# Regrouping the batches of a fused adaLN block (2, 4, 2 for 2, 2, 4), expert chunks of 2, 4, 1, 1 tiles, and the second modulations on ScalarE and GpSimd

## The reference

```python
mod = (_silu(L0_c) @ L0_wmod).reshape(L0_c.shape[0], 6, 1, -1)
sa, ca, ga, sb, cb, gb = (mod[:, 0], mod[:, 1], mod[:, 2], mod[:, 3], mod[:, 4], mod[:, 5])
ga = (2 * (ga >= 0) - 1) * jnp.maximum(jnp.abs(ga), 0.25)
gb = (2 * (gb >= 0) - 1) * jnp.maximum(jnp.abs(gb), 0.25)
h = _layernorm(x, axis=-1) * (1 + ca) + sa
x = x + ga * attn_ref(h, ...)
h = _layernorm(x, axis=-1) * (1 + cb) + sb
x = x + gb * ffn_ref(h, w_gate, w_up, w_down)

...
scores = (relu(x @ modr_w1 + modr_b1) @ modr_w2 + modr_b2)[..., 0]
topk_scores, topk_idx = jax.lax.top_k(scores, k)       
w = jax.nn.softmax(topk_scores, -1)
tok = take rows sorted(topk_idx); n1 = _ln(tok)
uv = n1 @ m_in_w; u, res = uv[:, :256], uv[:, 256:]
u = u * m_conv_w[:, 3] + m_conv_b; sp = u @ m_xproj_w
tok = tok + (u * (sp[:, 16:32].sum(-1) * sp[:, -1])[:, None] * silu(res)) @ m_out_w
n2 = _ln(tok); gate = top-2 softmax of n2 @ moe_r_w + moe_r_b, normalised
h1 = gelu(einsum('nd,edh->enh', n2, moe_w1) + moe_b1)
tok = tok + einsum('end,ne->nd', einsum('enh,ehd->end', h1, moe_w2) + moe_b2, gate)
out = x.at[..., sorted_idx].set(tok * w)

...
h = silu(fp4(x) @ fp4(w_gate).T) * (fp4(x) @ fp4(w_up).T)
y = fp4(h) @ fp4(w_down).T
```

## Time and profile before

| | |
|---|---|
| median of three runs | 245.74 us (245.60 to 245.93) |
| profiled execution, its own time | 245.69 us |
| its span, first to last instruction | 243.9 us |
| mean granted TensorE clock | 0.987 of full |
| busy: PE, PEld, DVE, ACT, POOL | 218.0, 176.6, 200.7, 131.7, 72.6 us |

### The profile page before, as it was taken

How to read it: one execution, slowest core, us unless ns; L and a number is a source line. 1 busy time by engine, 2 the same in 40 slices (tenths; PEclk the granted TensorE clock), 3 DMA queues, 4 the chain that set the end, 5 groups by cost and what they waited for, 6 DMA issues and landing times.

```text
span 243.9 us, 4519 instructions
## 1 busy us (share of the span) xinstructions
PE 218.0 (89%) x1431; PEld 176.6 (72%) x1436; DVE 200.7 (82%) x667; ACT 131.7 (54%) x343; POOL 72.6 (30%) x92
## 2 busy tenths in 40 slices
...
DMA packets 9126, 12.01 MB, mean 49 GB/s; under 512 B 1184, under 2 KB 5256, under 8 KB 9104
## 3 DMA queue, kind: packets, MB, share of 16 engines
...
q0 software_dynamic: 1024, 2.10, 2.9%
...
HBM read 10.65 MB, written 1.07 MB: 48 GB/s over the span
## 4 chain that ended last, share of the span: by engine, by line
DVE 40%; PE 32%; issue 11%; ACT 8%; POOL 4%; DMA 3%; SPq 1%; DVEq 0%; ACTq 0%; POOLq 0%
PE down_ps L1076 14%; PE up_ps L1076 9%; PE aux_ps L1076 8%; DVE acc L993 4%; DVE q_am L760 3%; DVE stats L730 3%; DVE qa L773 3%; POOL rstd L505 2%; ACT perm_m L604 2%; DMA wmod_s<-wmod_dram 2%; ACT h1T L669 2%; DVE hx L836 2%; DVE hh L1049 2%; DVE hh L1045 2%; DVE hx L829 2%
## 5 line engine op out<-in xcount | busy, mean ns | idle before, releaser
L669 ACT ACTIVATE h1T<-up_ps,par 128x256 f32<-128x256 f32 (+1 forms) x160 | 58.1, 434 | 40.8 <-PE up_ps L1076 32.6
L1076 PE MATMUL down_ps<-w_s,h1T 128*128 128x128 f32 x512 | 67.8, 280 | 5.2 <-DVE acc L993 4.3
L1076 PEld LDWEIGHTS down_ps<-w_s,h1T 128*128 128x128 f32 x512 | 63.5, 194 | 11.8 <-issue 9.9
L1076 PE MATMUL up_ps<-n2T,w_s 128*128 128x256 f32 (+1 forms) x320 | 66.3, 342 | 2.0 <-ACT h1T L669 2.0
L1076 PEld LDWEIGHTS up_ps<-n2T,w_s 128*128 128x128 f32 x320 | 49.7, 192 | 8.8 <-issue 4.9
L505 POOL TENSOR_TENSOR rstd<-veps,half_pow 128x2 f32<-128x2 f32 (+3 forms) x17 | 14.9, 875 | 83.9 <-DVE veps L735 83.9
L993 DVE SCALAR_TENSOR_TENSOR acc<-down_ps,gate,acc 128x128 f32<-128x128 f32 x64 | 20.2, 346 | 8.6 <-PE down_ps L1076 8.0
L1076 PE MATMUL aux_ps<-w_guT,h2T 128*128 128x352 f32 x64 | 21.4, 460 | 0.0
L1076 PE MATMUL up_ps<-lower,ones_b 128*128 128x512 bf16 x76 | 18.9, 379 | 0.5 <-issue 0.3
L558 ACT ACTIVATE qb<-qa 128x704 f32<-128x704 f32 (+5 forms) x20 | 11.3, 569 | 14.3 <-DVE qa L764 14.3
L543 POOL DMA_INDIRECT out_dram<-yo,row_ix x16 | 16.2, 1011 | 5.4 <-issue 2.4
...
## 6 DMA issues: line engine op xcount, KB each, us to landing
...
mod_r<-mod_dram SPq DMA_DIRECT2D x1, 768.0 KB, 4.7
...
```

The costliest lines, as they stand in the source:

```text
L669: last = A.activation(h1T[:, m % 2, hc, 0:n], up_ps[j % UP_BANKS][:, h * n:(h + 1) * n], ACT.Gelu, bias=col("moe_b1", e * HC + hc))
L1076: return nc.tensor.matmul(o, lhsT=l, rhs=r, start=start, stop=stop)
```

## The change

- Groups of 2, 4 and 2 batches; seven units in place of eight: `(0,1,0,2), (0,0,0,2), (1,1,2,4), (1,0,2,4), (2,1,6,2), (2,0,6,1), (2,0,7,1)`, as (group, half, first batch, tiles).
- Four expert chunks, of 2, 4, 1 and 1 tiles. In the 4-tile chunk an `up` fills a bank with one hidden slice of 512 rows, and there are 32 of them; `down_ps` holds four tiles and `acc` is four instructions.
- The second modulations: ScalarE copies them from PSUM (`mod.0.1` on ACT), GpSimd forms them in eleven instructions on 8 partitions, each waiting for the one before it; DVE no longer has the step.
- All four orders are written anew. `modh.0.1` is now ahead of `mod.0.0` on PE. The work of the routers, gates, experts and feed-forward tiles is the same in all, but cut differently: 177 DVE steps for 189, 57 POOL steps for 58, 171 ACT steps for 172, and the spare matmuls are 75 for 81.

The diff, with the orders cut to the places spoken of; of the three branches for `mod` the first added one is GpSimd's, the second ScalarE's, and the removed one DVE's:

```diff
-GROUPS = ((0, 2), (2, 2), (4, 4))
+GROUPS = ((0, 2), (2, 4), (6, 2))
-CHUNKS = ((0, 0, 2), (1, 2, 2), (2, 4, 2), (2, 6, 1), (2, 7, 1))
-UNITS = ((0, 1, 0, 2), (0, 0, 0, 2), (1, 1, 2, 2), (1, 0, 2, 2), (2, 1, 4, 4), (2, 0, 4, 2), (2, 0, 6, 1), (2, 0, 7, 1))
-ON_DVE = (6, 7)
+CHUNKS = ((0, 0, 2), (1, 2, 4), (2, 6, 1), (2, 7, 1))
+UNITS = ((0, 1, 0, 2), (0, 0, 0, 2), (1, 1, 2, 4), (1, 0, 2, 4), (2, 1, 6, 2), (2, 0, 6, 1), (2, 0, 7, 1))
+ON_DVE = (5, 6)
 PE_ORDER
-modh.0.0 mod.0.0-1 modh.0.1 spare.23.0 hT.0.0 ...
+modh.0.0-1 mod.0.0-1 spare.9.0 hT.0.0 ...
+... n2.0.0 scol.2.0 spare.1.11 up.0.0-1 logits.0.0 up.0.2 n1.1.0 up.0.3 down.0.0-1
+inproj.1.0 gateT.0.0 inproj.1.1 bias2.0.0 inproj.1.2 up.0.4 ...
+bias2.1.0 up.1.6-7
+down.1.0-1 h2T.1.0 up.1.8 down.1.2-3 up.1.9 gu.0.0 up.1.10-11 down.1.4-7 up.1.12-13 gu.0.1 up.1.14 down.1.8-11
+attn.2.0 up.1.15-16 soft.1.0 up.1.17-18 n2.2.0 up.1.19 logits.2.0 down.1.12-15 up.1.20 gu.1.0 up.1.21-22
+down.1.16 up.1.23 down.1.17-19 up.1.24 gateT.2.0 gu.1.1 bias2.2.0 h2T.2.0 up.1.25-26 down.1.20 up.1.27
+down.1.21-23 up.1.28-29 down.1.24 up.1.30 down.1.25-27 up.1.31 gu.2.0 down.1.28-31 wqT.0.2 up.2.0 hqT.0.0 gu.2.1
 DVE_ORDER
-silu.0.0 lnA.0.0 mod.0.0-1 lnB.0.0 wbc.0.0 lnC.0.0 lnA.1.0 lnB.1.0 lnA.2.0 scol.0.0 wM.0.0 rank.0.0 lnC.1.0
+silu.0.0 lnA.0.0 mod.0.0 lnB.0.0 lnC.0.0 lnA.2.0 lnA.1.0 lnB.1.0 scol.0.0 lnC.1.0 rank.0.0 lnC.1.1 pl.0.0
+wbc.0.0 lnB.2.0 n1A.0.0 ix.0.0 n1B.0.0 lnC.2.0 scol.1.0 ix.0.1 wM.0.0 rank.1.0 yA.0.0-1 pl.1.0 yB.0.0 mix.0.0
+pl.1.1 attn.0.0 n2A.0.0 smA.0.0 ix.1.0 n2B.0.0 n1A.1.0 ix.1.1 n1B.1.0 lgA.0.0 scol.2.0 lgB.0.0 rank.2.0 wq.0.0
+bias2.0.0 yA.1.0 acc.0.0 yA.1.1 wqb.0.0 wq.0.1 smB.0.0 acc.0.1 smA.1.0 mix.1.0 yB.1.0 pl.2.0 acc.0.2 attn.1.0
+n2A.1.0 wqb.0.1 n2B.1.0 ix.2.0 smD.0.0 smA.2.0 acc.0.3 n1A.2.0 fin.0.0 n1B.2.0 acc.0.4 lgA.1.0 fq.0.0 acc.0.5
+lgB.1.0 fqb.0.0 ix.2.1 acc.0.6 fin.2.0 wq.0.2 acc.0.7 fin.1.0 wqb.0.2 yA.2.0 mix.2.0 yA.2.1 fq.1.0 bias2.1.0
+fqb.1.0 fq.2.0 smB.1.0 acc.1.0 fin.4.0 fqb.2.0 yB.2.0 hh.0.0 acc.1.1 hh.0.1 hq.0.0 acc.1.2 attn.2.0 n2A.2.0
+hqb.0.0 n2B.2.0 smD.1.0 smB.2.0 lgA.2.0 acc.1.3 hh.1.0 lgB.2.0 acc.1.4 bias2.2.0 hh.1.1 hq.1.0 acc.1.5-6 hqb.1.0
+hh.2.0 acc.1.7 fin.3.0 hh.2.1 acc.2.0 fq.3.0 acc.2.1 hq.2.0 acc.2.2 hh.2.2 fqb.3.0 yo.0.0 hh.2.3 acc.2.3 hq.2.1
+acc.2.4 smD.2.0 hqb.2.0-1 acc.2.5 hh.3.0 yo.1.0 fq.4.0 hh.3.1 acc.2.6 hq.3.0 acc.2.7 fqb.4.0 fin.5.0 acc.3.0
+hh.3.2 hqb.3.0 acc.3.1 hh.3.3 fq.5.0 hq.3.1 hh.4.0 acc.3.2 hh.4.1 yo.2.0 fqb.5.0 acc.3.3 hq.4.0 acc.3.4 hqb.3.1
+yo.2.1 hh.5.0 acc.3.5 hqb.4.0 acc.3.6 hq.5.0 acc.3.7 fin.6.0 fq.6.0 yo.3.0 fqb.6.0 yo.3.1 hqb.5.0 hh.6.0 hq.6.0
+yo.4.0 hqb.6.0 yo.5.0 yo.6.0
 ACT_ORDER
+silu.0.0 modh.0.0-1 mod.0.1 hT.0.0 hr.0.0 ...
+... expc.0.0 perm.1.2 n2.0.0 perm.1.3
+gelu.0.0-1 expl.0.0 n1.1.0 sign.2.0 gelu.0.2 gateT.0.0 tanh.1.0-1 gelu.0.3 wqm.0.0 u.1.0 gelu.0.4-5 u.1.1
+... expc.1.0 fqm.1.0 u.2.0-1 gelu.1.6-7 expc.2.0 gelu.1.8 ...
 POOL_ORDER
-rsh.0.0 rsh.1.0 rsh.2.0 rs1.0.0 rs2.0.0 rs1.1.0 gather.1.0 gather.0.0-2 gather.1.1 gather.0.3 rs1.2.0 rs2.1.0
+rsh.0.0 mod.0.1 rsh.2.0 rsh.1.0 rs1.0.0 gather.0.0-3 rs2.0.0 gather.1.0 rs1.1.0 gather.1.1-7 wqs.0.0 rs2.1.0
...
+                elif kind == "mod":
+                    wait_aux_taken(pool, kind, a, i, 0)
+                    step_no = 0
+                    v = mod_s[:, CB * D:(CB + 1) * D]
+                    nc.gpsimd.tensor_scalar(v, v, 1.0, None, ALU.add)
+                    for m in (GA, GB):
+                        v, sign, size = mod_s[:, m * D:(m + 1) * D], mod_t[:, 0, :], mod_t[:, 1, :]
+                        nc.gpsimd.tensor_scalar(sign, v, 0.0, 2.0, ALU.is_ge, ALU.mult).then_inc(mod_step, 1)
+                        pool.wait_ge(mod_step, step_no + 1)
...
+                        last = nc.gpsimd.tensor_tensor(v, sign, size, ALU.mult)
...
+                    last.then_inc(mod_ready, 1)
...
+                elif kind == "mod":
+                    wait_aux_full(act, kind, a, i, 0)
+                    A.activation(mod_s[:, GA * D:], aux(kind, a, i, 0)[0:B, :], ACT.Copy
+                                 ).then_inc(aux_taken(kind, a, i, 0), 1)
...
-                    else:
-                        V.tensor_copy(mod_s[:, GA * D:], src[0:B, :]).then_inc(aux_taken(kind, a, i, 0), 1)
-                        wait_aux_taken(dve, kind, a, i, 0)
-                        v = mod_s[:, CB * D:(CB + 1) * D]
-                        V.tensor_scalar(v, v, 1.0, None, ALU.add)
-                        for m in (GA, GB):
...
-                        last.then_inc(mod_ready, 1)
```

100 lines of the change are left out of this document (41 added, 59 removed).

## The result

| | before | after |
|---|---|---|
| median | 245.93 us (245.60 to 247.86, 5 runs) | **250.44 us** (250.20 to 252.38, 5 runs) |
| ratio to before, 95% interval | | 1.0178 (1.0136 to 1.0219) |
| profiled execution: its time, span, clock | 245.69, 243.9 us, 0.987 | 252.38, 250.7 us, 0.979 |
| busy PE, PEld, DVE, ACT, POOL | 218.0, 176.6, 200.7, 131.7, 72.6 | 218.6, 165.1, 199.5, 126.7, 80.9 |

The change makes the kernel slower by 4.5 us, about 1.8%. The forecast was 248.8 us. The profiled execution of after is the slowest of its five, 1.9 us over the median; the clock rows further down show two half-clock stretches in it.

The account below looks back on a forecast made before the run. DVE bounds the kernel until the experts, then PE and DVE nearly full in step. DVE alone, PE alone in the four-tile chunk, DVE alone again: 162.8 + 78.6 = 241.4, +3.1 on 245.7 gives 248.8 us; 8 in 10: 242.5 to 253.3.

Parts of the forecast that it names:

- the case itself: The prediction's main case for the whole kernel: 248.8 us, own range 246.3 to 251.5, chance 0.6.
- Step 1: To the first expert: `scol.0.0` at 18.5 for 19.04 before, `n2B.0.0` 3.5 us later, `acc.0.0` at 56.0 for 61.98.
- Step 2: From `acc.0.0` to `fqb.1.0`, DVE alone sets the pace: 46.0 us of list plus waits, `h2T.1.0` at 103.5.
- Step 3: From `h2T.1.0` through the 4-tile chunk, PE alone sets the pace: 57.4 us plus 1.8, `acc.1.7` at 162.8.
- Step 4: From `acc.1.7` to the last DVE instruction, DVE alone sets the pace: 61.8 + 18.2 - 1.4 = 78.6 us.
- the sum: End of the last DVE instruction: 162.8 + 78.6 = 241.4 for 238.3 before, +3.1 us.
- Lists in step: Rival: unit 1 is delivered by 98, PE never waits ahead of `h2T.1.0`; 241.9 us, chance 0.2.
- Wash: Rival: DVE's idle in chunk 1 is half of that read, gain and loss cancel; 245.7 us, chance 0.1.
- Handover: Rival: in the 4-tile chunk a late `acc` holds PE, 0.6 us for each of eight experts; 253.6 us, chance 0.1.
- The moved modulations do nothing: Rival: ahead of the experts the spread read already binds `lnB.1.0`; 246.6 if landed by 14.1; no chance of its own.

Follow-up runs that it names:

- e5: After with 17 more DVE instructions whose result nobody reads, put behind `fin.3.0`, behind the four-tile chunk: 257.83 us, ratio to before 1.0436.
- e12: e1 with `wbc.0.0` moved to just ahead of `lnB.1.0` on DVE and `mod.0.0` ahead of `modh.0.1` on PE: 243.64 us, ratio to before 0.9898.
- e1: Before with only the second modulation moved to ACT and GpSimd, both halves of its product first on PE: 244.07 us, ratio to before 0.9926.
- e2: After with the second modulation moved back to DVE; groups, chunks and orders stay: 252.84 us, ratio to before 1.0283.
- e10: After with four `up` steps behind the four-tile chunk done twice on PE: 252.32 us, ratio to before 1.0277.
- e8: After with 17 more DVE instructions whose result nobody reads, put ahead of the four-tile chunk, behind `acc.0.3`: 257.98 us, ratio to before 1.0461.
- e9: After with four `up` steps of the four-tile chunk done twice on PE: 254.87 us, ratio to before 1.0332.
- e4: After with 17 more DVE instructions whose result nobody reads, put inside the four-tile chunk: 252.18 us, ratio to before 1.0247.
- e7: After with unit 2's work and the rest of unit 1's moved into the four-tile chunk, `yo.2.0` behind `fqb.4.0` on DVE: 256.10 us, ratio to before 1.0414.

## Why the prediction was right, and where its sizes were off

The sign and the mechanism held: slower, because DVE's list is short in the four-tile chunk and sets the pace ahead of it and behind it. The size was 1.4 us short, 3.1 forecast and 4.5 measured, inside the range of the case itself (246.3 to 251.5). By its own steps, for the times of the profiled execution:

| step | predicted | after | what was off |
|---|---|---|---|
| `mod.0.0` | 7.6 | 7.70 | |
| `scol.0.0` | 18.5 | 17.74 | the wait for the spread read |
| `n2B.0.0` | 43.0 | 42.15 | |
| first gelu; first expert's `down` ends | 46; 50.7 | 45.57; 50.75 | |
| `acc.0.0` | 56.0 | 55.46 | what is left of that wait |
| `h2T.1.0` on PE | 103.5 | 104.31 | the clock |
| `acc.1.7` | 162.8 | 164.21 | the clock; steps 1 and 3 cancel |
| last DVE instruction ends | 241.4 | 245.08 | the clock, and 0.6 in steps 3 and 4 each |

**Step 1.** I had the spread read issued at 11.6, because `mod.0.0` was later, and `lnB.1.0` waiting 2.2 us. It was issued at 10.73 and the wait was 0.69. In the fourteen profiled kernels `mod.0.0` started between 6.61 and 8.60 us and the read was issued between 10.07 and 10.81, and the one does not follow the other: in e5, where `mod.0.0` came last, at 8.60, the read was issued at 10.43. The read waits for the store to land, and e12's store, issued at 7.11, is followed by the read 3.34 us later; after's store was issued at 8.20, 2.53 us before the read. So a later `mod.0.0` did not move the read; that term was wrong, by 0.9 us, and the wait by 1.5. What sets the time at which the store lands, no run shows. `scol.0.0` and `n2B.0.0` came 0.8 us earlier than foretold, `acc.0.0` 0.5. GpSimd's eleven instructions took 6.64 us (9.60 to 16.24), 0.6 each from start to start and not 0.4; inside the bounds of 3 to 8. `rsh.1.0` ended at 18.94 and not 17.4; nothing waited. That the moved modulation is worth about 2 us to the end is shown by e1 and e2; of 2.8 us, I had left it 0.5 at `scol.0.0`.

**Step 2.** DVE's 46.0 us of list to `fqb.1.0` plus waits: `acc.0.0` to `h2T.1.0` was foretold at 47.5 us and took 48.85; in e10, which is the same kernel up to there and ran it at full clock, 47.55. That DVE sets this stretch is shown by e8: 5.65 us of DVE work there came out whole at `acc.1.7`. `lgB.1.0` took 3.01 us, for the 3.0 taken; 4.2 would have been the row's price with GpSimd beside it.

**Step 3.** `h2T.1.0` to `acc.1.7`: 59.3 us foretold, 59.90 measured (59.92 in e10). PE alone sets it (e9, e4). DVE idles 18.4 of 42 us from 123 to 165, where I had some 14 from `acc.1.2` on.

**Step 4.** 78.6 us foretold, 80.87 in the profiled execution, but 79.19 to 79.22 in four other kernels that are unchanged behind `acc.1.7` or change nothing that shows there (e2, e4, e9, e10). The difference is the clock. PE's share was said to fall under 85% until 225; it was 90% from 165 to 227 us. That mark was set too low, though DVE at 95% was the bound (e5: all of its 5.6 us; e10: none of PE's in the profiled run).

**DVE's whole work.** The forecast had DVE's list shorter by 4.7 us; busy time fell by 1.2, from 200.7 to 199.5. The time did not hang on that figure, since the sum was added up between fixed steps.

```profile
80.00:82.00 2.00, 2.00 (x10) 2.00 (x11) 1.83 (x8) 1.51 (x2) 0.00 (x0) 0.50 0.00 0
82.00:84.00 2.00, 2.00 (x12) 1.92 (x11) 0.77 (x3) 0.00 (x0) 0.00 (x0) 0.66 0.00 0
...
234.00:236.00 2.00, 2.00 (x7) 1.14 (x6) 1.19 (x4) 1.34 (x5) 1.70 (x3) 0.50 0.08 33
236.00:238.00 2.00, 2.00 (x10) 1.10 (x9) 1.41 (x4) 0.46 (x1) 1.34 (x2) 0.76 0.08 33
```

and of e10 over the same two places:

```profile
78.00:84.00 6.00, 4.75 (x34) 4.32 (x34) 5.63 (x20) 4.24 (x8) 0.73 (x1) 1.00 0.00 0
...
234.00:238.00 4.00, 3.53 (x24) 2.55 (x22) 3.57 (x9) 0.93 (x3) 3.08 (x4) 1.00 0.08 33
```

From `acc.0.0` to `acc.1.7` e10 needs 107.47 us for after's 108.75, and from `acc.1.7` to the last DVE instruction (242.02) 79.21 for 80.87, with more PE work and not less. So the two half-clock stretches cost 1.28 and 1.66 us, 2.9 together. Ahead of each of them PE had waited, 1.14 and 2.26 us; e10 has the same waits and kept its full clock. Without the two stretches after's DVE would end at 242.1, by this estimate; the sum said 241.4. What is left, 0.7 us, is the error of the sum without the clock, and part of its smallness is luck: the start was put 0.5 too late, steps 3 and 4 were each 0.6 too short.

**The rivals.** Lists in step: fell, `h2T.1.0` came at 104.3 and not below 100. Wash: fell. Handover: 2.8 us of PE's waits in the whole kernel for 4.3 in before; fell for after, but e7 shows that it is there for another order. The moved modulations do nothing: fell by e1 and e2.
